# A hybrid block on one core: the first four units spread by TensorE, the last feed-forward product in four parts, three exponential buffers, new places

## The chip, the core and the metric

One core of a Trainium2 chip runs the whole program. Its engines are TensorE (PE, matmuls into PSUM), VectorE (DVE), ScalarE (ACT), GpSimd (POOL) and SyncE (SP, which here only issues DMAs). They run side by side and wait for each other by semaphores. PSUM has eight banks of 128 x 512 fp32. The metric is the time of one execution on the device in microseconds; the median of several runs counts.

## What is computed

The input x has 4 batches of 1024 rows and 128 channels. Three kinds of layer follow each other, each behind a layer norm and added to x:

```
x = x + attn(layernorm(x), Wq, Wk, Wv, Wo)          # 16 heads of 8; window of 32 and every 64th key, causal
x = x + ffn(layernorm(x), k0, k1, k2, s0, s1, s2)   # 256 -> 512 -> 512 -> 128, weights +1 or -1, relu * 2
x = x + mamba(layernorm(x), ...)                    # itself x + res_scale * out
x = x + ffn(layernorm(x), k0, k1, k2, s0, s1, s2)   # the same weights again

# mamba: 256 inner channels, 16 states, over 1024 steps
u, z = split(norm(x) @ W_in);  u2 = silu(conv(u) + conv_b)
dt_lo, B, C = split(u2 @ W_xp);  dt = softplus(dt_lo @ W_dt + b_dt)
h[t] = exp(dt[t] * A) * h[t-1] + (dt[t] * u2[t]) * B[t];  y[t] = sum over states of h[t] * C[t]
out = ((y + u2 * D) * silu(z)) @ W_out
```

## The kernel before

The work is cut by batches b and by halves of 512 rows (m = 2b + h, eight of them). Attention of a batch runs in 24 units u, with 128 x 512 scores each. A feed-forward pass f covers 512 rows (there are 17, the last two of half the size): transposed rows, first layer (fl1, four products over mo), second layer (fl2, four outputs mo with 8 fp16 matmuls each), last product (fl3, fp32) and the sum into X (fl3_v).

The scan of a half runs in 32 units, 256 in all. A unit holds 8 channels x 16 states on 128 partitions and 512 steps. For each unit: dt8_d reads the channels' step sizes from DRAM, spread over 16 partitions each, into DT (6 slots, NT); du8_d does the same for the inputs dt * u2 into D (12 slots, ND). decay_s (ACT, L1574) makes exp(dt * A) in one of the banks 0 and 1. The drive multiplies the inputs by B: drive_v on DVE (L1252), for 9 of 32 units drive_p on POOL (L1739). scan_v (DVE, L1264) runs the recurrence in place; out_p (POOL, L1752) multiplies two units by C; csum_t (PE, L951) sums over states into bank 2. Ahead of it stands, for each half and block eb of 128 channels: dt_t (PE, L936), dt_s, dt_v, dt_p, dr_v (the sizes, in sR), du_p (POOL, L1732, sR * u2, in sE), and dt_d and du_d, which write sR and sE to DRAM, from where dt8_d and du8_d read.

In an attention unit asc_t makes the scores (L764 the mask, L787 or L792 the products), asc_v (DVE, L1134, L1140) the maxima and for odd units the shift, asb_t (PE, L806) the shift of even units, asc_s (ACT, L1411) the exponentials into Sx, atr_t (PE, L815) the transposes, atr_s (ACT, L1418) their copy into PT, and apv_t (L832) the products with the values. Sx and PT have two buffers each. warm_t (L998) are idle products of two constants, whose result nobody reads.

The order of the instructions of each engine is written out: PLACES holds for each step a list of numbers, one for each time it occurs (a place), WARM the idle products as (place, bank, how many). timetable() sorts all by number, and each engine issues its own steps in that order. No engine goes past a step that waits. The products of PE take their banks in turn from a ring, from dt_t(0, 0) on the four banks 4 to 7; the turn waits until the bank's last content was read.

The last product of a pass waits for all four outputs of the second layer:

```
bank = bank_of["fl3", i] = turn((v_fx, i + 1))
eng.wait_ge(s_f2, 4 * i + 4)
for k in range(N // 128):
    for ki in range(4):
        t = eng.matmul(bank[:, 128 * k:128 * k + 128], h1[:, ki, 128 * k:128 * k + 128], w2[:, ki, :],
                       start=(ki == 0), stop=(ki == 3))
```

## Time and profile before

| | |
|---|---|
| median of 3 runs | 799.41 us (798.85 to 801.10) |
| the profiled execution | 800.71 us |
| its span, first to last instruction | 798.9 us |
| instructions | 22483 |
| busy: PE, DVE, ACT, POOL | 710.9, 689.1, 617.5, 601.3 us |
| mean granted clock of PE | 0.981 |
| moved by DMA | 154.95 MB, mean 194 GB/s |

A window of the trace gives the busy time of each engine in a stretch, the granted clock of PE as a share of 2.4 GHz, and what DMA moved. A row of the timeline is one instruction or a run of the same ones, with its start, its length and, in brackets, how long the engine was idle before it and which engine's work ended that. The chain is followed back from the last instruction. An fp32 matmul stands in the trace as two PE instructions. A line number is that of the kernel before; in the changed kernel the same code stands 15 to 46 lines further down.

### The profile page before, as it was taken

To read this page: it belongs to the slowest core of one execution; us is meant where nothing else is said; L and a number is where in the kernel's file an instruction comes from. 1 tells how busy PE (TensorE), PEld (TensorE's weight loads), DVE (VectorE), ACT (ScalarE), POOL (GpSimd) and SP (SyncE) were. 2 spreads that over 40 slices of the span, in tenths; PEclk is the share of its full clock that TensorE was granted. 3 is DMA by queue.
4 is the path that set the end of the run, shared out by engine and by line. 5 is a ranking of instruction groups with operands and counts; after the bars stand their busy time and mean duration, and the time that the engine had idled before them with its cause. 6 is when DMAs were issued, how large, how long until landed. Compare 5 with 4: busy or idle time off the path is not lost. (4 is left out here: it accounts for less than half of the span.)

```text
span 798.9 us, 22483 instructions
## 1 busy us (share of the span) xinstructions
PE 710.9 (89%) x8144; PEld 420.1 (53%) x8144; DVE 689.1 (86%) x1145; ACT 617.5 (77%) x1227; POOL 601.3 (75%) x591
## 2 busy tenths in 40 slices
PE   7998998998789999999999998998998989697788
PEld 5675655645565446547555364445454555262346
DVE  6887127999999989999899989999999898798983
ACT  4775789889769998999689989887778656754533
POOL 3032345879988989769897799799798999898671
PEclk9999999999999999999999999999999999798989
DMA  6000019997987769786968799978897989899860
GB/s 204 3 3 2 2 45 244 255 236 224 269 218 198 176 173 270 202 216 184 232 185 237 215 241 255 229 222 242 222 248 215 269 245 256 225 244 255 213 156 27
DMA packets 84176, 154.95 MB, mean 194 GB/s; under 512 B 9433, under 2 KB 10082, under 8 KB 84066
## 3 DMA queue, kind: packets, MB, share of 16 engines
q1 hardware_dynamic: 84066, 153.51, 71.7%
q8 instruction: 65, 1.06, 0.6%
q14 instruction: 45, 0.37, 0.2%
HBM read 142.47 MB, written 11.01 MB: 192 GB/s over the span
## 5 line engine op out<-in xcount | busy, mean ns | idle before, releaser
L1752 POOL TENSOR_TENSOR d<-d,cr 128x1024 f32<-128x1024 f32 x128 | 300.4, 2354 | 34.1 <-DVE d L1264 24.4
L1574 ACT ACTIVATE ps<-dt,An 128x512 f32<-128x512 f32 x256 | 173.7, 690 | 53.6 <-DVE d L1264 39.8
L1264 DVE TENSOR_TENSOR_SCAN d<-ps,hl,d 128x512 f32<-128x512 f32 x128 | 157.8, 1267 | 8.6 <-ACT ps L1574 7.1
L1264 DVE TENSOR_TENSOR_SCAN d<-ps,d 128x512 f32<-128x512 f32 x128 | 150.5, 1206 | 7.4 <-ACT ps L1574 4.4
L877 PE MATMUL ps<-h,w 128*128 128x512 f16 (+1 forms) x512 | 121.8, 392 | 11.2 <-DVE h L1208 9.6
L1252 DVE TENSOR_TENSOR d<-ps,d 128x512 f32<-128x512 f32 x184 | 118.4, 673 | 2.1 <-DMA d<-dud 1.9
L1739 POOL TENSOR_TENSOR d<-d,br 128x512 f32<-128x512 f32 x72 | 91.4, 1276 | 13.2 <-DMA d<-dud 13.1
L877 PEld LDWEIGHTS ps<-h,w 128*128 128x128 f16 x512 | 49.1, 101 | 85.8 <-DVE h L1208 21.7
L951 PE MATMUL ps<-d,cst 128*32 128x512 f32 x512 | 70.5, 625 | 11.4 <-POOL d L1752 8.3
L815 PE MATMUL ps<-cst,sx 128*128 128x128 f32 x384 | 55.4, 279 | 10.9 <-ACT sx L1411 5.5
L888 PEld LDWEIGHTS ps<-w,h 128*128 128x128 f32 x496 | 56.7, 192 | 7.8 <-ACT h L1477 6.1
L888 PE MATMUL ps<-w,h 128*128 128x128 f32 x496 | 58.9, 277 | 1.8 <-ACT h L1477 1.8
L916 PE MATMUL ps<-xnT,Wk 128*128 128x512 f32 x128 | 56.9, 594 | 1.7 <-ACT xnT L1509 0.9
L1418 ACT COPY pt<-ps 128x512 f32<-128x512 f32 x96 | 53.4, 590 | 5.8 <-PE ps L815 3.6
L815 PEld LDWEIGHTS ps<-cst,sx 128*128 128x128 f32 x384 | 41.8, 141 | 28.6 <-issue 9.4
L1477 ACT ACTIVATE h<-ps 128x512 f32<-128x512 f32 (+1 forms) x64 | 35.7, 580 | 23.1 <-PE ps L877 22.7
L998 PEld LDWEIGHTS ps<-cst 128*128 128x128 f32 x352 | 44.4, 199 | 15.8 <-issue 9.2
L1134 DVE TENSOR_REDUCE mn<-ps 128x8 f32<-128x512 f32 x64 | 41.4, 679 | 12.9 <-PE ps L792 12.7
L998 PE MATMUL ps<-cst 128*128 128x128 f32 x352 | 48.4, 288 | 4.5 <-DMA cst<-in_w 4.5
L832 PEld LDWEIGHTS ps<-v,pt 128*32 128x32 f32 x3072 | 34.1, 110 | 31.8 <-issue 29.2
L1397 ACT COPY v<-ps 32x256 f32<-32x256 f32 (+1 forms) x96 | 41.9, 436 | 11.2 <-PE ps L742 6.2
L832 PE MATMUL ps<-v,pt 128*32 128x18 f32 (+1 forms) x3072 | 39.8, 191 | 8.9 <-issue 3.2
(177 smaller groups left out, 1337.7 us busy)
## 6 DMA issues: line engine op xcount, KB each, us to landing
dt<-dtd SPq DMA_DIRECT2D x256, 256.0 KB, 5.3
d<-dud SPq DMA_DIRECT2D x256, 256.0 KB, 5.3
dtd<-sR SPq DMA_DIRECT2D x16, 256.0 KB, 3.6
dud<-sE SPq DMA_DIRECT2D x16, 256.0 KB
X<-in_x SPq DMA_DIRECT2D x8, 256.0 KB, 6.1
br<-bcd SPq DMA_DIRECT2D x8, 256.0 KB, 3.3
cr<-bcd SPq DMA_DIRECT2D x8, 256.0 KB, 3.7
out<-X SPq DMA_DIRECT2D x3, 512.0 KB, 5.6
```

Source lines behind the costliest of these rows:

```text
L815: t = eng.transpose(bank[:, 128 * k:128 * k + 128], sx[:, 128 * k:128 * k + 128], ident)
L832: t = eng.matmul(bo[32 * j:32 * j + 32, at, a, :], pt[:, i, 32 * j:32 * j + 32], V[:, 2 * kk + w, :, 4 * (2 * c + a) + j, :], start=True, ...
L877: t = eng.matmul(bank[:, 0:N], w1[:, ki, 128 * mo:128 * mo + 128], h0[:, s, ki, 0:N], start=(ki == s == 0), stop=(ki == 3 and s == 1))
L888: t = eng.matmul(bank[:, 128 * k:128 * k + 128], h1[:, ki, 128 * k:128 * k + 128], w2[:, ki, :], start=(ki == 0), stop=(ki == 3))
L916: t = eng.matmul(bank[:, :], Wk[:, k, 128 * eb:128 * eb + 128], xnT[:, 1 + k:513 + k], start=(k == 0), stop=(k == KC - 1))
L951: t = eng.matmul(bank[32 * q:32 * q + 32, :], csel[:, 24 - 8 * w:56 - 8 * w], D[:, (4 * k + q) % ND, :], start=(w == 0), stop=(w == 3))
L998: eng.matmul(banks[k][:, 0:128], ident, ident, start=True, stop=True)
L1252: eng.tensor_tensor(d, PB[:, :], d, ALU.mult).then_inc(v_dr, 1)
L1264: eng.tensor_tensor_scan(d, banks[u % NG][:, :], d, hl[:, r:r + 1] if m % 2 else 0.0, ALU.mult, ALU.add).then_inc(v_sc, 1)
L1574: eng.activation(banks[u % NG][:, :], DT[:, u % NT, :], ACT.Exp, scale=An[:, g:g + 1]).then_inc(s_da, 1)
L1739: eng.tensor_tensor(d, d, BR[m % 2][:, :], ALU.mult).then_inc(p_dr, 1)
L1752: eng.tensor_tensor(d, d, CR[m % 2][:, :].unsqueeze(1).to_broadcast((128, n, 512)), ALU.mult).then_inc(p_cm, n)
```

## The change

It has five parts.

1. For the units 0 to 3 (FIRST = 4) the step sizes and inputs no longer go through DRAM. A constant "spread" is added; bdt_t and bdu_t multiply 32 partitions of it with the same 32 of sR or sE, so that a bank holds what dt8_d or du8_d would have brought. decay_s reads the one bank, drive_v the other, all four drives are on DVE (those of units 0 and 1 were on POOL). dt8_d and du8_d run from unit 4 on.
2. fl3_t is cut in four parts, one for each output of the second layer, each with its own wait and its own place; the bank is taken by the first.
3. Sx and PT have three buffers (NS).
4. The idle products are set anew: 35 groups with 238 products, 33 groups with 176 before.
5. All places are new.

```
+FIRST = 4
+def driver(u):
+    return "v" if u < FIRST or u % NR not in DRIVEN_P else "p"
+def landed(u, n):
+    return u // n + 1 - (u % n < FIRST)
...
-    (CORE, 'decay_s dt8_d du8_d scan_v'),
+    (CORE, 'decay_s scan_v'),
+    (CORE[FIRST:], 'dt8_d du8_d'),
+    (CORE[:FIRST], 'bdt_t bdu_t'),
...
+    put("spread", (p[:, None] % 32 == p[None, :] % 8).astype(np.float32))
...
-        Sx = [sb(f"sx{i}", [128, 512]) for i in range(2)]
-        PT = [sb(f"pt{i}", [128, 4, 128]) for i in range(2)]
+        NS = 3
+        Sx = [sb(f"sx{i}", [128, 512]) for i in range(NS)]
+        PT = [sb(f"pt{i}", [128, 4, 128]) for i in range(NS)]
...
-            def fl3_t(f):
+            def fl3_t(f, mo):
...
-                bank = bank_of["fl3", i] = turn((v_fx, i + 1))
-                eng.wait_ge(s_f2, 4 * i + 4)
+                if mo == 0:
+                    bank_of["fl3", i] = turn((v_fx, i + 1))
+                eng.wait_ge(s_f2, 4 * i + mo + 1)
                 for k in range(N // 128):
...
+                    t = eng.matmul(bank_of["fl3", i][:, 128 * k:128 * k + 128], h1[:, mo, 128 * k:128 * k + 128], w2[:, mo, :],
+                                   start=(mo == k == 0), stop=(mo == 3), skip_group_check=True)
+                if mo == 3:
+                    t.then_inc(t_f3, 1)
...
+            def bdt_t(u):
+
+                bank = bank_of["bdt", u] = turn((s_da, u + 1))
+                eng.wait_ge(v_md, 2)
+                q = slice(32 * u, 32 * u + 32)
+                eng.matmul(bank[:, :], spread[q, :], sR[q, :], start=True, stop=True).then_inc(t_bdt, 1)
+
+            def bdu_t(u):
+
+                bank = bank_of["bdu", u] = turn((v_dr, u + 1))
+                eng.wait_ge(p_md, 3)
+                q = slice(32 * u, 32 * u + 32)
+                eng.matmul(bank[:, :], spread[q, :], sE[q, :], start=True, stop=True).then_inc(t_bdu, 1)
...
+                if u < FIRST:
+
+                    eng.wait_ge(v_set, V_END)
+                    eng.wait_ge(l_br, 32)
+                    eng.wait_ge(t_bdu, u + 1)
+                    eng.tensor_tensor(d, bank_of["bdu", u][:, :], BR[0][:, :], ALU.mult).then_inc(v_dr, 1)
+                    return
...
+                if u < FIRST:
+                    eng.wait_ge(t_bdt, u + 1)
+                    src = bank_of["bdt", u]
```

The waits of asc_v, asc_s and atr_s look back three units in place of two. The next dr_v waits until all four bdt_t are done, the next dt_s until all bdu_t are.

**First place: DVE around the first scans.** L1134, L1140 and L1150 are attention of batch 1, L1236 and L1245 the sizes, L1202 and L1208 feed-forward pass 1, L1252 drives, L1264 scans. Before:

```order
L1134 TENSOR_REDUCE zf<-ps 128x2x8
L1140 TENSOR_TENSOR sx<-ps,zf 128x512
L1236 TENSOR_SCALAR sT<-sE 128x512
L1264 SCALAR_TENSOR_TENSOR d<-ps,d 128x512 x2
L1202 TENSOR_TENSOR h<-ps,h 128x512
L1245 SCALAR_TENSOR_TENSOR sR<-ps,sL 128x512
L1252 TENSOR_TENSOR d<-ps,d 128x512 x2
L1208 SCALAR_TENSOR_TENSOR h<-ps,h 128x512 x3
L1264 SCALAR_TENSOR_TENSOR d<-ps,d 128x512 x2
```

In the changed kernel (L1287 the drives of the first four units, L1291 the other drives, L1303 scans, L1180, L1164 and L1170 the attention, L1266 sizes):

```order
L1287 TENSOR_TENSOR d<-ps,br 128x512
L1303 SCALAR_TENSOR_TENSOR d<-ps,d 128x512
L1287 TENSOR_TENSOR d<-ps,br 128x512 x3
L1303 SCALAR_TENSOR_TENSOR d<-ps,d 128x512 x3
L1180 STREAM_TRANSPOSE fc<-zf 128x256 x2
L1164 TENSOR_REDUCE zf<-ps 128x2x8 x2
L1170 TENSOR_TENSOR sx<-ps,zf 128x512
L1266 TENSOR_SCALAR sT<-sE 128x512
L1291 TENSOR_TENSOR d<-ps,d 128x512 x3
```

Four drives and four scans now stand ahead of the second round of reductions and of the sizes' second block; five more drives and all of pass 1's first layer stand between scan 3 and scan 4.

**Second place: PE in the same stretch.** L998 are idle products, L843 the attention's output, L815 and L832 transposes and value products, L764 and L787 scores, L806 the shift. Before:

```order
L843 MATMUL ps<-wgt,jt 128x128 x4
L806 MATMUL ps<-zf,cst 128x512
L998 MATMUL ps<-cst 128x128 x5
L815 MATMUL ps<-cst,sx 128x128 x8
L832 MATMUL ps<-v,pt 32x4x9 x32
L764 MATMUL ps<-masks,e 128x512 x2
L787 MATMUL ps<-KD,qm 64x2x32 x32
L737 MATMUL ps<-cst,lna 128x128 x2
L806 MATMUL ps<-zf,cst 128x512
L815 MATMUL ps<-cst,sx 128x128 x8
```

In the changed kernel (L959 is bdt_t, L966 bdu_t, L1028 the idle products):

```order
L1028 MATMUL ps<-cst 128x128 x7
L959 MATMUL ps<-sR,cst 128x512
L847 MATMUL ps<-v,pt 32x4x9 x32
L959 MATMUL ps<-sR,cst 128x512
L779 MATMUL ps<-masks,e 128x512 x2
L802 MATMUL ps<-KD,qm 64x2x32 x32
L966 MATMUL ps<-sE,cst 128x512
L821 MATMUL ps<-zf,cst 128x512
L959 MATMUL ps<-sR,cst 128x512
L966 MATMUL ps<-sE,cst 128x512 x3
L830 MATMUL ps<-cst,sx 128x128 x8
L959 MATMUL ps<-sR,cst 128x512
```

The eight new products stand in six places between those of the attention, four of them ahead of the transposes of units 2 and 3.

**Third place: PE in the last fifty microseconds**, from the first layer of pass (3, 2, 0) on. L866 is the first layer, L877 the second, L951 the sum over states, L981 the last half's output product, L998 idle. Before:

```order
L998 MATMUL ps<-cst 128x128 x3
L866 MATMUL ps<-h,w 128x512 x8
L951 MATMUL ps<-d,cst 32x512 x4
L877 MATMUL ps<-h,w 128x512 x8
L951 MATMUL ps<-d,cst 32x512 x4
L877 MATMUL ps<-h,w 128x512 x24
L981 MATMUL ps<-w,u 128x128 x8
```

In the changed kernel (L881, L892, L981 and L1011 are the same four, L1028 idle):

```order
L1028 MATMUL ps<-cst 128x128 x4
L881 MATMUL ps<-h,w 128x512 x6
L1028 MATMUL ps<-cst 128x128 x9
L881 MATMUL ps<-h,w 128x512 x2
L1028 MATMUL ps<-cst 128x128 x10
L892 MATMUL ps<-h,w 128x512 x8
L1028 MATMUL ps<-cst 128x128 x15
L981 MATMUL ps<-d,cst 32x512 x4
L1028 MATMUL ps<-cst 128x128 x8
L981 MATMUL ps<-d,cst 32x512 x4
L892 MATMUL ps<-h,w 128x512 x24
L981 MATMUL ps<-d,cst 32x512 x4
```

Four more groups of idle products stand between the layers and the sums over states. In the first pass the scores (L764, L792) that stood between the second layer and the last product now stand ahead of the second layer. On SP the first reads of inputs, eight in a row, stand ahead of the first five reads of sizes; before, the two kinds alternated by twos and threes.

## Rows read from the trace of the kernel before

**Rows 1.** Windows: length, busy of PE, PEld, DVE, ACT, POOL; clock, DMA, GB/s.

```profile
0.00:125.00 125.00, 110.90 (x1842) 75.36 (x1842) 73.77 (x214) 88.22 (x194) 40.71 (x81) 1.00 0.15 49
125.00:775.00 650.00, 580.56 (x6157) 328.40 (x6143) 606.88 (x906) 521.48 (x1013) 557.47 (x502) 0.98 0.86 228
775.00:799.00 24.00, 19.48 (x164) 16.32 (x160) 8.44 (x25) 7.82 (x22) 3.12 (x8) 0.99 0.07 23
...
75.00:100.00 25.00, 24.67 (x252) 14.83 (x251) 6.04 (x16) 15.97 (x37) 7.01 (x18) 1.00 0.01 3
```

**Rows 2.** Timeline around the first scan: start, length, engine, line, operation, idle before.

```profile
117.61 1.28 POOL L1732 TENSOR_TENSOR sE<-sR,u 128x512 f32<-128x512 f32 x1 [0.80 <-DVE sR L1245]
...
123.14 1.16 SPq L686 DMA_DIRECT2D d<-dud  x2
126.35 2.50 POOL L1739 TENSOR_TENSOR d<-d,br 128x512 f32<-128x512 f32 x2 [3.03 <-DMA d<-dud]
129.94 2.33 DVE L1264 TENSOR_TENSOR_SCAN d<-ps,d 128x512 f32<-128x512 f32 x2
...
141.88 5.67 DVE L1264 TENSOR_TENSOR_SCAN d<-ps,d 128x512 f32<-128x512 f32 x5
```

**Rows 3.** A product dt_t in the timeline; eight convolution products on the chain.

```profile
111.18 1.09 PE L936 MATMUL ps<-lnm,Wdt 9*128 9x512 f32 x2 [0.42 <-ACT lnm L1538]
...
589.22 7.14 PE ps L916 x16
```

**Rows 4.** Scans and drives on DVE: ns of one, least, median, most.

```profile
L1264 DVE TENSOR_TENSOR_SCAN d<-ps,d x128: 1181/1209/1224, 129.9 to 704.6; 128x512 f32<-128x512 f32 x128
...
L1252 DVE TENSOR_TENSOR d<-ps,d x184: 626/677/692, 133.5 to 770.3; 128x512 f32<-128x512 f32 x184
```

**Rows 5.** Windows before the first scan, columns as in rows 1.

```profile
110.00:120.00 10.00, 8.20 (x161) 5.88 (x164) 3.59 (x10) 7.92 (x18) 5.24 (x5) 1.00 0.29 95
120.00:130.00 10.00, 8.47 (x178) 5.45 (x169) 5.81 (x16) 9.35 (x23) 4.97 (x8) 1.00 0.80 221
```

**Rows 6.** Idle before L888 and before L1418: until whom, us, times.

```profile
  ACT h L1477: 8.0, 8
...
  PE ps L832: 1.9, 3
```

**Rows 7.** Timeline of the first pass' second layer, last product, and what follows.

```profile
74.39 7.42 PE L877 MATMUL ps<-h,w 128*128 128x512 f16 x32
...
82.97 3.84 PE L888 MATMUL ps<-w,h 128*128 128x128 f32 x32
...
88.93 0.20 POOL L1710 TENSOR_SCALAR mr<-mmv 128x4 f32<-128x4 f32 x1 [17.20 <-DVE mmv L1018]
```

**Rows 8.** Timeline at the end: the last products of the last two passes.

```profile
792.41 1.95 PE L888 MATMUL ps<-w,h 128*128 128x128 f32 x16
792.62 0.39 ACT L1477 ACTIVATE qm<-ps 128x256 f32<-128x256 f32 x1 [0.49 <-PE ps L877]
```

**Rows 9.** Windows in which the granted clock is low, columns as in rows 1.

```profile
695.00:700.00 5.00, 4.24 (x11) 1.09 (x11) 5.00 (x8) 2.96 (x6) 4.49 (x4) 0.55 0.97 257
...
735.00:740.00 5.00, 5.00 (x20) 2.06 (x19) 1.97 (x3) 2.36 (x4) 2.19 (x1) 0.79 0.71 177
...
765.00:770.00 5.00, 5.00 (x18) 1.92 (x19) 5.00 (x5) 2.95 (x6) 5.00 (x4) 0.72 1.06 278
```

**Rows 10.** Pieces of the chain that ended last: start, us, engine, line, instructions.

```profile
569.29 7.02 PE ps L877 x32
...
706.61 2.90 PE ps L998 x26
...
731.56 8.93 PE ps L877 x28
```

**Rows 11.** Waits that nothing in the profile explains: us, times, longest us.

```profile
PEld ps L832 <- issue: 29.2, 54, 1.6
...
PEld ps L916 <- issue: 28.6, 116, 0.8
```

More of the change, by code:

```diff
@@ L23 @@
 CONST, NCONST = {}, 0
-for _name, _n in (("ident", 128), ("qmask", 4), ("csel", 56), ("one8", 1), ("rmask", 2)):
+for _name, _n in (("ident", 128), ("qmask", 4), ("csel", 56), ("one8", 1), ("rmask", 2), ("spread", 128)):
     CONST[_name] = (NCONST, _n)
@@ L98 @@
 DRIVEN_P = [0, 1, 5, 9, 13, 17, 21, 25, 29]
-def driver(r):
-    return "p" if r in DRIVEN_P else "v"
+FIRST = 4
+def driver(u):
+    return "v" if u < FIRST or u % NR not in DRIVEN_P else "p"
 def driven(u, by):
-    return u // NR * sum(driver(r) == by for r in range(NR)) + sum(driver(r) == by for r in range(u % NR))
+    return sum(driver(x) == by for x in range(u))
+def landed(u, n):
+    return u // n + 1 - (u % n < FIRST)
 def rows_of(f):
@@ L165 @@
     (BATCH_HALVES[2:], 'aln_v'),
-    ([(u,) for u in range(NCORE) if driver(u % NR) == "v"], 'drive_v'),
+    ([(u,) for u in range(NCORE) if driver(u) == "v"], 'drive_v'),
     (BLOCKS[:-1], 'gate_p yev_v'),
@@ L170 @@
     (BATCHES, 'aap_p akp_p'),
-    ([(u,) for u in range(NCORE) if driver(u % NR) == "p"], 'drive_p'),
+    ([(u,) for u in range(NCORE) if driver(u) == "p"], 'drive_p'),
     (PAIRS, 'out_p'),
@@ new lines @@
+    "dt_d": [113425, 141515, 180593, 210290, 271266, 290303, 353024, 387904, 439657, 458170, 505869, 544136, 592186, 622015, 671561,
+        692352],
+    "dt_p": [108041, 128368, 176237, 193326, 267819, 282512, 349577, 381280, 436210, 454211, 499855, 521343, 588739, 613711, 663358,
+        680096],
+    "dt_s": [106237, 126564, 174273, 190652, 266015, 280058, 347200, 379476, 434406, 450904, 497816, 518533, 586730, 609305, 661175,
+        674950],
+    "dt_t": [105083, 125410, 172709, 189498, 264861, 278678, 346046, 378322, 433252, 449750, 496662, 517379, 585576, 608151, 660021,
+        673423],
@@ new lines @@
+    "jrec_v": [54404, 101414, 206452, 252936, 360000, 376022, 529030, 597673],
+    "jsub_p": [50292, 88764, 184030, 247009, 337633, 369290, 511222, 587438],
+    "jsum_p": [53249, 99796, 204659, 251335, 356344, 374376, 520264, 596182],
+    "jtr_v": [58941, 107911, 211559, 258000, 366902, 386442, 536731, 606332],
+    "jx_v": [60945, 111370, 216511, 262806, 371764, 391528, 538653, 608389],
+    "lg_v": [751325, 751667],
+    "lm_t": [751809, 752256],
+    "lm_v": [752453, 753633],
+    "lmo_t": [748155, 749045],
@@ new lines @@
+    "lpre_p": [720809],
+    "mln_p": [83973, 148557, 244002, 294859, 410981, 459343, 562604, 637007],
+    "mln_s": [88821, 154887, 248961, 300602, 415846, 472845, 568082, 641378],
+    "mln_t": [88527, 154172, 248527, 300077, 415506, 472140, 568261, 641532],
+    "mln_v": [82682, 146581, 242353, 292727, 409690, 458052, 561313, 635716],
+    "mno_s": [86748, 151332, 246777, 297924, 413756, 468771, 565379, 639782],
+    "mout_t": [218347, 291850, 382829, 459439, 563687, 620002, 695437],
+    "mout_v": [221838, 293933, 385799, 461522, 568662, 624329, 698659],
@@ L475, in const @@
             return cst[0:rows, at:at + n]
-        ident, qmask, csel, one8, rmask = (const(n) for n in ("ident", "qmask", "csel", "one8", "rmask"))
+        ident, qmask, csel, one8, rmask, spread = (const(n) for n in ("ident", "qmask", "csel", "one8", "rmask", "spread"))
         masks = sb("masks", [128, 288], BF16)
@@ L879, in fl2_t @@
                 t.then_inc(t_f2, 1)
-            def fl3_t(f):
+            def fl3_t(f, mo):
                 i = FFN_AT[f]
                 _, _, _, h1, N = room(f)
-                bank = bank_of["fl3", i] = turn((v_fx, i + 1))
-                eng.wait_ge(s_f2, 4 * i + 4)
+                if mo == 0:
+                    bank_of["fl3", i] = turn((v_fx, i + 1))
+                eng.wait_ge(s_f2, 4 * i + mo + 1)
                 for k in range(N // 128):
-                    for ki in range(4):
-                        t = eng.matmul(bank[:, 128 * k:128 * k + 128], h1[:, ki, 128 * k:128 * k + 128], w2[:, ki, :],
-                                       start=(ki == 0), stop=(ki == 3))
-                t.then_inc(t_f3, 1)
+                    t = eng.matmul(bank_of["fl3", i][:, 128 * k:128 * k + 128], h1[:, mo, 128 * k:128 * k + 128], w2[:, mo, :],
+                                   start=(mo == k == 0), stop=(mo == 3), skip_group_check=True)
+                if mo == 3:
+                    t.then_inc(t_f3, 1)
             def mln_t(m):
@@ L1119, in asc_v @@
                 nw = 8 if kind else 4
-                bank, sx = bank_of["sc", b, u], Sx[U % 2]
+                bank, sx = bank_of["sc", b, u], Sx[U % NS]
                 sv = bank[:, :].rearrange("p (a w k) -> p a w k", a=2, w=nw)
```

232 lines of the change are left out of this document (107 added, 125 removed), and 319 rows, old and new, of tables (PLACES, WARM).

## The prediction

> **What bounds the kernel now.** I first read the busy times of the engines in three long stretches [rows 1]. Up to 125 us VectorE (DVE) is busy 73.8 us and TensorE (PE) 110.9. From 125 to 775 us DVE is busy 606.9 of 650 us, PE 580.6, GpSimd (POOL) 557.5 and ScalarE (ACT) 521.5. The last 24 us hold short products and small steps. In the window from 75 to 100 us PE is busy 24.67 of 25 and DVE 6.04 [rows 1]. So PE and the attention chains set the time up to the first scan, and after it the list of DVE does, with 256 scans and a drive for most of them. The queues run in the order written by the table of places: a hole of one engine is filled only if the table puts work there. Of DVE's 110 us of idle time, 51 lie before 125 us (125 - 73.8), 43 between 125 and 775 (650 - 606.9), 15.6 behind.
>
> **Part 1, units 0 to 3 on another way.** Their sizes and inputs now go from sR and sE to DRAM and come back spread over 128 partitions. In the trace sE is ready at 117.61 + 1.28 = 118.9 us, the first read of inputs is issued at 123.14, POOL's first drive starts at 126.35 after 3.03 us of waiting, the first scan at 129.94 [rows 2]. In the changed kernel one product with "spread" puts each tile into a bank: 118.9 plus one product. The nearest row for one with few rows of contraction is that of dt_t, 9 rows high: 1.09 us with its latency [rows 3]. So drive 0 can start near 120.0 and scan 0 near 120.8, nine us earlier. That is not nine us of gain, since the work only moves into DVE's holes. Moved are four scans and the drives 2 and 3: 4 x 1.209 + 2 x 0.677 = 6.2 us [rows 4]; drives 0 and 1 come anew from POOL, 1.35 us. Together 7.5 us have to go between 120 and 130 us, where DVE is idle for 10 - 5.8 = 4.2 us [rows 5]. 3.3 us of other DVE work (the score reductions of batch 1, and pass 1) is pushed behind 130. Net 6.2 - 3.3 = **2.9 us**. Bounds: 6.2 if holes before 120 take the rest, 0 if PE can't deliver (a rival, below).
>
> PE gets 8 products more. Back to back such a product takes 0.89 us (16 instructions, 8 products, in 7.14) [rows 3], 7.1 us in all, in a stretch from 110 to 130 where it is idle for 20 - 16.7 = 3.3 us [rows 5]. So its own queue comes 3.8 us late there. That is the same 3 to 4 us of attention and pass 1 that DVE pushes back anyway; the two overlap, and I count them once. POOL loses two drives, which is free, because it waited for them [rows 2]. On SyncE (SP) the eight first reads of inputs now stand ahead of the sizes of unit 4. First read to first drive took 3.2 us [rows 2]; if each read behind it adds 1.2 us (256 KB at the 221 GB/s of the window from 120 to 130 [rows 5]), unit 4's sizes land at about 122 + 3.2 + 9.6 = 135 us. Scan 4 started at 141.88 [rows 2]: covered by some 6 us.
>
> **Part 2, the last product in four parts.** The matmuls stay in number. What goes is PE's wait for the fourth activation: ahead of L888 PE was idle for 8.0 us in 8 cases until h of L1477 was there [rows 6]. In the first pass attention scores fill that wait: the last L877 runs out at 74.39 + 7.42 = 81.8, L888 starts at 82.97, and POOL stands idle 17.20 us until the sums behind it are there [rows 7]. In the changed kernel these scores stand ahead of the second layer and the first part can follow at once: **1.2 us** earlier. Bounds 0 and 1.2, since PE is full there [rows 1] and the order decides who profits. In later passes DVE is mostly the late one: of the 8.0 us I take **0.5**, bounds 0 and 6. At the very end nothing: PE runs L888 from 792.41 on without a hole, the fourth activation (792.62) is covered by the other pass's products [rows 8]. Against it: the bank is held from the first part on, one of four in the ring.
>
> **Part 3, three buffers for exponentials.** The wait this can take away is that of the copy L1418 for L832 two units back, 1.9 us in 3 cases [rows 6]. I take **0.5**, bounds 0 and 1.9, and, if freer orders bring more, 3.
>
> **Part 4, idle products.** 176 become 238, nearly all new ones in the last sixth: from place 641,000 on 56 before and 117 now. The granted clock shows what they meet: 0.55 from 695 to 700 us, 0.79 from 735 to 740, 0.72 from 765 to 770 [rows 9]. On the chain a second-layer instruction takes 219 ns at full clock (32 in 7.02) and 319 in the stretch from 731.56 (28 in 8.93), 2.8 us more [rows 10]. In the two other stretches DVE is busy 5.00 of 5, so a faster PE gives little there; from 735 to 740 it is busy 1.97 [rows 9], so the 2.8 can be had. The bound is three such stretches, 8.4. The price: an idle product is two instructions, 0.223 us (26 in 2.90, on the chain) [rows 10]; with 6 more on the path 1.3. Net **1.5 us**, bounds 8.4 gained and, with all 61 on the path, 13.6 lost.
>
> **The other places.** Many rows of the four queues change places by a few. No row prices this; I take 0, and 3 us to both sides for the range.
>
> **The sum.** 2.9 + 1.2 + 0.5 + 0.5 + 1.5 = 6.6 us. The profiled execution took 800.7 us, so 794.1; it lies 1.3 above the median of 799.4, so the forecast is **792.8 us**.
>
> **The rivals.** *The scans keep their whole lead* (A): 6.2 for part 1, and 2.8 for part 4 with no price. 6.2 + 1.2 + 0.5 + 0.5 + 2.8 = 11.2 gives 788.2. For it: DVE is busy only 3.59 of the 10 us before 120 [rows 5]. Against it: the inputs don't exist before 118.9.
>
> *PE can't deliver the spread tiles* (B). They are products of 32 rows between products of 128. Where the shape of the tile changes PE stands with nothing to wait for: 29.2 us in 54 cases before L832, 0.54 a time, against 28.6 in 116, 0.25, before L916, whose shape stays [rows 11]. The eight stand in six places of the queue: 3 us more on top of the 3.8. Attention of batch 1 and pass 1 then come 7 us late, which eats part 1's 6.2. With part 4 at 0 the sum is 6.2 - 7 + 1.2 + 0.5 + 0.5 = 1.4, the time 798.0: no change. Against it: dt_t, 9 rows high between 128-row products, took 1.09 us as a whole [rows 3]. The Trainium skill has a rule for this (TensorEngine Tiling (Array Packing), Key Properties): changing the tiling mode drains TensorE, while tiles of one mode work in parallel. By that rule the eight cost six drains, and the three that stand in a row are nearly free, which takes 2 us off. The gap before L832 agrees with a drain; no row here shows 32-row tiles side by side.
>
> *The idle products lie on the path* (C), the case that ends slower. Near the end four groups of 9, 10, 15 and 8 stand directly ahead of first- and second-layer products and sums. If what comes behind is ready by then, PE works them off first. All 61 are 13.6 us; against gains of 2.9 + 1.2 + 0.5 + 0.5 + 2.8 = 7.9 that is 5.7 slower, 805.1. It turns slower by 0.3% once more than 46 of the 61 (10.3 us) are on the path. For it: 13 are on the chain now [rows 10]. Against it: PE is idle 69 us from 125 to 775 [rows 1], so most can lie in holes.
>
> **How the numbers follow.** The forecast 0.53, A 0.20, B 0.15, C 0.12. A measurement of this kernel can tell about 0.3% from no change, 2.4 us. Forecast and A are faster, B within, C mostly slower; a little of the forecast's case and of C falls within 0.3%: faster 0.73, same 0.16, slower 0.11. The forecast's own range is 789.5 to 796.5. For 8 in 10 it goes down to 787.5, which takes in A, and up to 799.5, which takes in B.
>
> **What would show it.** Part 1: first scan at 119 to 123 us, the fifth not before 133; DVE's hole between 115 and 125 filled; its idle time from there to the last scan near the 43 us of now, and the last scan some 6 us earlier. Part 2: L903 (L888 before) in the first pass right behind the second layer. Part 4: clock above 0.9 in the windows from 685 to 770, and 219 ns for a second-layer instruction. It is wrong if PE has no hole from 110 to 130 and DVE waits for reductions there (B), if idle products have more than 4 us on the chain (C), or if the scans' lead at unit 32 is gone at unit 200: then the new places lost elsewhere what the first units gained.

## The result, and the profile after

The changed kernel takes **810.67 us** (median of 4 runs, 807.97 to 813.30), the kernel before 799.82 beside it: 1.0134 of it, 95% interval 1.0086 to 1.0182. It is 11 us slower, where 6.6 us less were forecast. Its runs lie in two groups, 808 us at a mean granted clock of 0.976 to 0.979 and 813 us at 0.964 to 0.966. The profiled execution is one of the first (808.20 us, span 806.4, which is 7.5 more than before).

The three long stretches, as [rows 1] (length, busy of PE, PEld, DVE, ACT, POOL; clock, DMA, GB/s):

```profile
0.00:125.00 125.00, 113.25 (x1818) 76.38 (x1818) 76.39 (x226) 88.61 (x196) 39.26 (x82) 1.00 0.16 50
125.00:775.00 650.00, 590.89 (x6263) 345.16 (x6264) 598.63 (x891) 513.39 (x1003) 550.06 (x497) 0.97 0.84 223
775.00:799.00 24.00, 20.49 (x165) 15.56 (x163) 14.47 (x31) 10.29 (x25) 8.86 (x11) 1.00 0.18 60
```

From 125 to 775 us DVE is busy 598.6 us, 8.3 less than before: new holes, not new work. They are few. Worked out from both traces, the start of each scan less its place in the table (in us) is the lag of the plan:

```
                     scan 4 (start)   last scan (start)   jumps of the lag by over 3 us
kernel before         5.2  (141.9)    16.7  (772.2)       none
changed kernel       11.6  (147.1)    31.7  (779.9)       7.1 at scan 4, 3.7 at scan 98 (399), 3.5 at scan 222 (given back), 4.7 at scan 252 (775)
```

The new table puts the last scan 7 us earlier; execution loses 15 us more against it than before, in three places.

**The first units.** The timeline of the changed kernel around scans 0 to 4, by start, length, engine, line, and idle time before:

```profile
122.95 1.32 PE L966 MATMUL ps<-sE,cst 32*128 32x512 f32 x6
126.57 1.12 PE L959 MATMUL ps<-sR,cst 32*128 32x512 f32 x2
129.28 1.16 PE L802 MATMUL ps<-KD,qm 64*64 64x64 f32 x64
135.17 1.86 PE L952 MATMUL ps<-lnm,Wdt 9*128 9x512 f32 x2 [4.73 <-issue]
...
126.01 3.69 DVE L1303 TENSOR_TENSOR_SCAN d<-ps,d 128x512 f32<-128x512 f32 x3
138.51 0.43 DVE L1266 TENSOR_SCALAR sT<-sE 128x512 f32<-128x512 f32 x1 [5.95 <-ACT sE L1590]
147.05 2.33 DVE L1303 TENSOR_TENSOR_SCAN d<-ps,d 128x512 f32<-128x512 f32 x2
...
137.15 0.60 ACT L1588 ACTIVATE sE<-ps 128x512 f32<-128x512 f32 x1 [6.18 <-PE ps L952]
```

The spread products do what was wanted: 1.12 us for one alone, three in a row in 1.32, scans 0 to 3 done by 129.7 us, where before [rows 2] two were done by 132.3. Then PE stands for 4.73 us ahead of dt_t(0, 1) (L952), with "issue" as the reason: the profile shows no semaphore that it waits for. ACT and DVE wait 6 us for it, and scan 4 starts 5.2 us later than before. Behind the hole PE also runs slower; L952 takes 1.86 us, not 1.09 as in [rows 3]. The windows there:

```profile
125.00:130.00 5.00, 4.46 (x128) 3.14 (x132) 4.86 (x7) 4.27 (x11) 2.44 (x2) 1.00 1.06 256
130.00:135.00 5.00, 0.44 (x32) 0.48 (x23) 2.35 (x5) 0.95 (x3) 2.62 (x3) 0.83 1.05 258
135.00:140.00 5.00, 4.61 (x8) 1.53 (x7) 1.49 (x3) 2.04 (x4) 0.98 (x1) 0.50 0.09 22
```

After 0.44 us of PE in 5 the granted clock falls to 0.50 of 2.4 GHz, its level of 1.2. DMA was full until the hole ended. The DMA view of 119 to 133 us (reads with KB each and us from issue to landing), and of 132.3 to 132.6 (packets, MB, share):

```profile
d<-dud SPq DMA_DIRECT2D x8, 256.0 KB, 5.1
dt<-dtd SPq DMA_DIRECT2D x5, 256.0 KB, 8.7
```

```profile
q1 hardware_dynamic: 46, 0.08, 115.1%
q8 instruction: 1, 0.02, 26.2%
```

Thirteen reads are issued from 120.7 to 128.9 us. By their landings 8 of them are under way at most (at 128 us) and 5 at 132.3, and among their packets is one of kind "instruction", which starts at 132.35 us, 2.8 us before PE goes on. The page counts 66 of this kind on queue q8. Two later holes of this kind are in the middle of work that waits for nothing, the second inside one group of 64 matmul records (an fp32 product is two):

```profile
217.04 1.12 PE L821 MATMUL ps<-mn,cst 128*128 128x512 f32 x2 [1.93 <-issue]
...
386.63 0.44 PE L847 MATMUL ps<-v,pt 128*32 128x18 f32 x31
389.27 0.76 PE L847 MATMUL ps<-v,pt 128*32 128x18 f32 x33 [2.19 <-issue]
```

An earlier one of 1.86 us stands where no data moves. The DMA view of 51 to 57 us has a single packet, one of instructions, and then PE's row:

```profile
DMA packets 1, 0.02 MB, mean 3 GB/s; under 512 B 0, under 2 KB 0, under 8 KB 0
...
56.28 0.61 PE L847 MATMUL ps<-v,pt 128*32 128x18 f32 x45 [1.86 <-issue]
```

**The end.** PE, SP and DVE from 761 us on, and two windows:

```profile
761.57 1.89 PE L892 MATMUL ps<-h,w 128*128 128x512 f16 x4 [3.38 <-DVE h L1238]
763.25 4.26 PE L1028 MATMUL ps<-cst 128*128 128x128 f32 x30
767.44 1.06 PE L981 MATMUL ps<-d,cst 128*32 128x512 f32 x8
768.43 2.05 PE L1028 MATMUL ps<-cst 128*128 128x128 f32 x16
...
768.57 2.61 SPq L701 DMA_DIRECT2D d<-dud  x3
...
772.77 0.69 DVE L1291 TENSOR_TENSOR d<-ps,d 128x512 f32<-128x512 f32 x1 [3.58 <-DMA d<-dud]
775.18 2.45 DVE L1303 TENSOR_TENSOR_SCAN d<-ps,hl,d 128x512 f32<-128x512 f32 x2
```

```profile
760.00:765.00 5.00, 3.43 (x13) 2.47 (x14) 5.00 (x7) 2.41 (x6) 2.76 (x2) 0.66 0.87 209
765.00:770.00 5.00, 5.00 (x45) 4.04 (x44) 4.19 (x5) 2.48 (x5) 4.36 (x3) 1.00 0.04 9
```

Fifteen idle products (L1028) stand ahead of a sum over states (L981) and take 4.26 us. The sum releases D's buffers; only then, at 768.57, SP issues the last reads of inputs, and DVE waits for them. DMA's share from 765 to 770 us is 0.04; the same window of before has 1.06 [rows 9]. That is the mechanism of rival C, near the end alone.

### The profile page after: what moved, and what is told of

Read it like the earlier page. It is cut to its first block and busy times, and to the rows that moved or that the text cites. A ratio compares the mean times of both kernels' runs of the same rounds, so it can differ in the third digit from the quotient of the medians.

```text
span 806.4 us, 22760 instructions
## 1 busy us (share of the span) xinstructions
PE 729.3 (90%) x8284; PEld 441.3 (55%) x8284; DVE 690.0 (86%) x1147; ACT 613.8 (76%) x1227; POOL 598.2 (74%) x589
## 5 line engine op out<-in xcount | busy, mean ns | idle before, releaser
L1620 ACT ACTIVATE ps<-dt,An 128x512 f32<-128x512 f32 x252 | 170.7, 691 | 59.9 <-DVE d L1303 43.1
L1303 DVE TENSOR_TENSOR_SCAN d<-ps,hl,d 128x512 f32<-128x512 f32 x128 | 157.8, 1266 | 4.4 <-ACT ps L1620 2.6
L1303 DVE TENSOR_TENSOR_SCAN d<-ps,d 128x512 f32<-128x512 f32 x128 | 150.5, 1206 | 6.5 <-ACT ps L1620 4.9
L892 PE MATMUL ps<-h,w 128*128 128x512 f16 (+1 forms) x512 | 118.0, 382 | 7.3 <-DVE h L1238 6.7
L1291 DVE TENSOR_TENSOR d<-ps,d 128x512 f32<-128x512 f32 x182 | 117.3, 671 | 5.9 <-DMA d<-dud 5.9
L1785 POOL TENSOR_TENSOR d<-d,br 128x512 f32<-128x512 f32 x70 | 88.8, 1275 | 19.9 <-DMA d<-dud 16.1
L892 PEld LDWEIGHTS ps<-h,w 128*128 128x128 f16 x512 | 47.6, 99 | 80.9 <-DVE h L1238 17.5
L981 PE MATMUL ps<-d,cst 128*32 128x512 f32 x512 | 69.6, 619 | 7.7 <-POOL d L1798 7.2
L1028 PEld LDWEIGHTS ps<-cst 128*128 128x128 f32 x476 | 59.4, 200 | 18.2 <-issue 10.2
L1028 PE MATMUL ps<-cst 128*128 128x128 f32 x476 | 63.4, 287 | 5.3 <-DMA cst<-in_w 5.3
L903 PEld LDWEIGHTS ps<-w,h 128*128 128x128 f32 x496 | 58.5, 193 | 8.4 <-issue 5.3
L903 PE MATMUL ps<-w,h 128*128 128x128 f32 x496 | 60.4, 278 | 0.9 <-ACT h L1516 0.7
L1164 DVE TENSOR_REDUCE mn<-ps 128x8 f32<-128x512 f32 x64 | 41.3, 678 | 5.1 <-PE ps L807 4.9
L1450 ACT ACTIVATE sx<-ps 128x512 f32<-128x512 f32 x48 | 28.4, 591 | 21.3 <-PE ps L821 21.0
L1238 DVE SCALAR_TENSOR_TENSOR h<-ps,h 128x512 f16<-128x512 f32 (+1 forms) x64 | 39.4, 662 | 6.0 <-ACT h L1510 5.8
```

The costliest lines, as they stand in the source:

```text
L892: t = eng.matmul(bank[:, 0:N], w1[:, ki, 128 * mo:128 * mo + 128], h0[:, s, ki, 0:N], start=(ki == s == 0), stop=(ki == 3 and s == 1))
L903: t = eng.matmul(bank_of["fl3", i][:, 128 * k:128 * k + 128], h1[:, mo, 128 * k:128 * k + 128], w2[:, mo, :], start=(mo == k == 0), stop=( ...
L981: t = eng.matmul(bank[32 * q:32 * q + 32, :], csel[:, 24 - 8 * w:56 - 8 * w], D[:, (4 * k + q) % ND, :], start=(w == 0), stop=(w == 3))
L1028: eng.matmul(banks[k][:, 0:128], ident, ident, start=True, stop=True)
L1291: eng.tensor_tensor(d, PB[:, :], d, ALU.mult).then_inc(v_dr, 1)
L1303: eng.tensor_tensor_scan(d, banks[u % NG][:, :], d, hl[:, r:r + 1] if m % 2 else 0.0, ALU.mult, ALU.add).then_inc(v_sc, 1)
```

## Where PE stands: one position of its code

The trace has one 16 KB instruction packet on q8 for every 256 records of PE (17032 records, 66 packets; matmuls, weight loads and semaphore waits counted). So I numbered PE's records in order and added up its idle time by position modulo 256. In the changed kernel position 193 holds 11.6 us, the next one 3.4, apart from the wait for the first inputs at the very start. Every hole above stands there: the one at 56 us ahead of record 7 x 256 + 193, at 135 us 15 x 256 + 193, at 217 us 22 x 256 + 193, at 389 us 39 x 256 + 193. In none of the 20 traces (the two kernels and the 18 experiments below) does PE get past record 256 n + 193 sooner than 2.2 us behind the start of packet n; after a hole of over 0.9 us it goes on 2.3 to 3.3 us behind. In the kernel before the same position holds 2.5 us. All idle time of PE that the profile puts down to "issue" is 4.8 us before and 13.6 after.

The traces also hint at when a packet is asked for. No packet n starts more than 42 records ahead of record 256 (n - 1) + 193, and in the median it starts 1.0 to 2.2 us behind it (19 traces; 0.5 in the one whose mean clock is 0.554); so the next packet is asked for, as far as this tells, about when PE gets past the boundary before. Ahead of the hole near 135 us the packet started 4.7 us behind that record, while PE worked the 256 records off in 2.9 us.

**Theory, late code**: PE's instructions arrive by the same DMA engines as the data, 256 at a time. If PE works through a dense stretch (many short products), it runs out of instructions, the more so when reads of data hold the packet up. Where it runs out is set by the count of all instructions ahead, so any edit moves it. **Rivals**: the eight spread products hold PE up (B); idle products are the whole loss (C).

## Experiments: the two causes

All times are set beside runs of the kernel before on the same chip; the chip differs between groups of experiments, so the ratios compare better than the times; "of before" is the ratio with its 95% interval. P193 is the idle time at that position in the run's trace.

**Reads drawn apart.** Four of the eight first du8_d behind the sizes, and in dt8_d:

```
+                if u == 6:
+                    eng.wait_ge(v_sc, 4)
```

> The changed kernel with the first reads of SyncE drawn apart: four of the eight first reads of inputs (units 8 to 11) stand behind the reads of sizes, and the third read of sizes waits for the fourth scan, so that some six reads of 256 KB and not thirteen are outstanding between 121 and 131 us. Late code (PE's packets of instructions queue behind the data): PE's hole of 4.7 us ahead of dt_t(0, 1) (L952) shrinks below 1.5 us, scan 4 starts near 142 and not 147 us, and the median falls by 5 to 7 us, to 804 to 806. PE can't deliver the spread tiles (B): hole and time stay within 1 us. Idle products on the path: nothing changes here, since it acts near 765 us.

Measured: 808.99 us, 1.0106 of before (1.0060 to 1.0152). The hole ahead of dt_t(0, 1) is gone (P193 7.2 us), scan 4 starts at 145.2. The time fell by 1.7 us and not by 5 to 7, with intervals that overlap. In the profiled run PE was at half clock from 117 to 134 us, and a spread product took 2.07 us, so that scan 3 came 3 us later. At that clock PE needed 4.0 us for the 256 records ahead of the boundary and not 2.9, so this run alone doesn't show that the reads made the hole. The run with both edits below does: full clock up to 132 us, the same reads, and 1.71 us of hole.

**Idle group out.**

```
-    (735961, 2, 15), (739046, 4, 8), (757905, 5, 4),
+    (739046, 4, 8), (757905, 5, 4),
```

> The changed kernel without the group of 15 idle products ahead of csum_t(60), nothing else. Idle products on the path: the 4.3 us of these products at a clock of 0.66 vanish, the last reads of inputs are issued some 4 us earlier and the median falls by 4 to 5 us, to 806 or 807. If they buy clock for what stands behind them, the sums and layers behind run slower by as much and the time stays within 1 us. Late code: the hole near 135 us stays as it is; since 30 instructions fewer come at 765 us, no boundary of a packet before that moves.

Measured: 809.62 us, 1.0120 (1.0061 to 1.0179). That can't be told from the changed kernel; 4 to 5 us less were expected. In its trace the plan's lag jumps by 1.5 us at scan 252, not 4.7: the end is repaired, and more was lost ahead of it (the runs spread from 806 to 815 us). A second expectation missed: nothing differs ahead of 765 us, and yet the hole near 135 us did not stay as it was:

```profile
134.13 1.86 PE L952 MATMUL ps<-lnm,Wdt 9*128 9x512 f32 x2 [1.33 <-issue]
```

PE was at half clock there from 124.0 to 144.5 us and needed 4.9 us for the 256 records. Scan 4 started at 148.1, later than with the hole of 4.73. So one trace says little on the length of a hole, and here a slow PE cost scan 4 as much as a hole.

**Boundary moved by taking 13 idle products out.**

```
-    (8848, 2, 8), (10191, 0, 3), (102142, 5, 5), (108670, 7, 6), (111520, 2, 7), (197534, 4, 1), ...
+    (8848, 2, 8), (10191, 0, 3), (102142, 5, 5), (197534, 4, 1), ...
```

> The changed kernel without the 13 idle products at the places 108,670 and 111,520, which fed nothing: 52 PE instructions (each product stands for a weight load and a matmul, in fp32 two of each) fewer ahead of dt_t(0, 1), so that every later packet of 256 instructions begins 52 instructions further on in the program. Late code: the hole of 4.7 us no longer stands ahead of dt_t(0, 1) (L952) but some 50 instructions behind it or is much smaller, the holes in the value products at 389 us and ahead of the shift at 217 us move as well, and the median changes by 2 to 6 us, likely down. If PE waits for a semaphore or for the drain of a changed tile shape at L952, the hole stays ahead of L952 with its 4 to 5 us. Idle products on the path: within 1 us.

Measured: 815.43 us (four runs within 1.4), 1.0186 (1.0152 to 1.0219). The hole ahead of L952 is gone; holes now stand at 165.3 us (1.77) and 397.0 (2.31), again at 193 (P193 7.9 us). The direction of the time was missed, for another reason. The windows from 110 us, and a spread product:

```profile
110.00:115.00 5.00, 2.85 (x18) 1.82 (x16) 1.05 (x2) 4.94 (x12) 2.85 (x3) 1.00 0.41 118
115.00:120.00 5.00, 3.92 (x68) 1.64 (x68) 3.34 (x12) 2.85 (x8) 3.79 (x9) 0.75 0.29 108
120.00:125.00 5.00, 5.00 (x70) 2.90 (x70) 2.29 (x4) 2.37 (x5) 1.93 (x5) 0.50 0.74 204
...
118.03 2.07 PE L959 MATMUL ps<-sR,cst 32*128 32x512 f32 x2
```

Without these idle products PE is busy 2.85 us of 5 and the clock falls to half just where the first units run; the time is 4.8 us longer (this median less that of the changed kernel), with 3.7 us less at P193. That the missing products made the clock fall isn't shown. The run with the reads apart has all of them, PE is busy 4.65 of 5 us from 110 to 115, and the clock fell at the same place:

```profile
115.00:120.00 5.00, 5.00 (x134) 3.29 (x134) 2.26 (x10) 2.47 (x6) 4.34 (x12) 0.69 0.30 108
120.00:125.00 5.00, 5.00 (x10) 1.79 (x10) 3.10 (x4) 2.82 (x8) 0.05 (x1) 0.50 0.87 221
```

**Both edits together.**

> The reads drawn apart and the group of 15 idle products taken out, together. Both causes hold and are independent: 5 to 7 and 4 to 5 us less than the changed kernel, near 799 us, which is the time of the kernel before. Only one of the two holds: 803 to 807.

Measured: 801.55 us (10 runs), 1.0019 (0.9997 to 1.0040): 9 us less than the changed kernel, between the 799 expected of two causes and the 803 to 807 of one. They don't add up as independent causes would: alone the edits gave 1.7 and 1.1 us. No run shows why. The half clock may be part of it: the profiled runs of the two single edits had 17 and 20 us of it near 130 us, this one 3.4. P193 is 11.0 us, hardly less than the 11.6 of the changed kernel, so the sum of the holes doesn't set the time by itself. Scan 4 starts at 141.9, as before. What is left of the first hole:

```profile
130.94 1.01 PE L954 MATMUL ps<-lnm,Wdt 9*128 9x512 f32 x2 [1.71 <-issue]
```

## Experiments: the same order, another boundary

These add tiny products of constants and change nothing else. Behind the first idle group of the kernel before, 36 of them (144 instructions), or 16 (64):

```
+                if (k, products) == (2, 8):
+                    for _ in range(36):
+                        eng.matmul(banks[k][0:32, 0:8], ident[0:32, 0:32], ident[0:32, 0:8], start=True, stop=True)
```

> The kernel before with 36 tiny products of constants (32x32 by 8 columns, four PE instructions each) behind its first group of idle products, while PE waits for input anyway: 144 PE instructions more ahead of everything, no order, wait or buffer changed. In the traces so far PE's stalls without a semaphore stand at instruction 256 n + 193 of its stream, whatever the kernel, and each ends 2.5 to 2.8 us behind the start of a 16 KB packet of instructions. In the kernel before PE's own work takes over 4 us from instruction 256 n - 64 to 256 n + 193 in all but one or two places; moved by 144 there are several dense stretches (transposes, value products, scores) at that spot. Late code: the stalls at 256 n + 193 sum to 6 us or more (2.5 us in the kernel before) and the time rises by 3 to 8 us. If the order or waits make the stalls: at most 1.5 us more, the price of the 144 tiny instructions.

> The kernel before with 16 tiny products (64 PE instructions, 1.1 us) at the same spot. Late code: the stalls at 256 n + 193 rise from 2.5 to 6 us or more, and the time by 4 to 12 us, since of the shifts worked out from the trace all from 40 to 230 put dense stretches ahead of the boundary. If 144 was an odd case: 801 to 803.

Measured: with 144 instructions **825.26 us**, 1.0367 (1.0312 to 1.0421), P193 17.8 us; with 64, 811.27 us, 1.0160 (1.0138 to 1.0182), P193 7.5 us. The tiny products themselves cost 2.9 us with 144 (the scores of unit 0 start at 19.09, not 16.21) and nothing with 64 (16.18). With 144 the loss is far above the 3 to 8 us expected. The hole near 135 us stands inside one group of 64 score products (L787). First the run with 144, then with 64:

```profile
131.27 0.56 PE L787 MATMUL ps<-KD,qm 64*64 64x64 f32 x18
137.84 1.55 PE L787 MATMUL ps<-KD,qm 64*64 64x64 f32 x46 [6.01 <-issue]
```

```profile
128.87 1.14 PE L787 MATMUL ps<-KD,qm 64*64 64x64 f32 x58
133.17 0.34 PE L787 MATMUL ps<-KD,qm 64*64 64x64 f32 x6 [3.16 <-issue]
```

Behind the 18th matmul record of the group the one time, behind the 58th the other: 40 matmuls, each with its weight load, make 80 records, which is 144 - 64. No wait, shape or bank can do that. This settles where PE stands.

> The changed kernel with 36 tiny products (144 PE instructions) behind its first idle group, just as in the kernel before that went from 800 to 825 us. If the old order only stands at a lucky boundary and the new one is otherwise as good: 810 to 825 us, no slower than 825. If the new order is worse by itself by the 10 us of the main result: 835 us or so.

Measured: the changed kernel with 144 takes 814.93 us, 1.0202 (1.0175 to 1.0230), P193 9.6. At this boundary the changed kernel is 10 us faster than the kernel before (13 by the two ratios), with 8.2 us less at P193; at its own it is 11 us slower. The kernel before stands at a good boundary: both its shifts are slower by 11 and 25 us, those of the changed kernel by 4 and 7.

> The changed kernel with 12 such tiny products behind the idle group at place 111,520: 48 PE instructions more from 112 us on, nothing else. Late code: PE's stalls ahead of L952 (4.7 us), at 217 us (1.9) and at 389 us (2.2) vanish or shrink below 1 us, since the spots 256 n + 193 then come behind longer stretches; one near 397 us may come in their place. The median falls by 4 to 8 us. Otherwise: no change beyond 1 us. Idle products on the path near 765 us: untouched, 4 to 5 us stay.

> The changed kernel with all three edits: first reads drawn apart, the group of 15 idle products out, 48 PE instructions more from 112 us on. Late code: of the stalls at 256 n + 193 of the version without the shift (1.6 us at 131, 2.5 at 214, 1.6 at 289, 1.9 at 389, 0.7 at 397, at least 7 us) most go, of which DVE passes on 3 to 5 us, for 797 to 799 us: faster than the kernel before. If alignment of the code doesn't matter: 801 to 802 us as without the shift.

Measured: 817.80 us, 1.0241 (1.0201 to 1.0280), and 812.92 us, 1.0150 (1.0110 to 1.0190). Both expectations missed. The first hole went as expected (scan 4 at 144.6), but the boundary fell into another dense group (P193 14.3 and 13.7 us). In the first of the two:

```profile
392.46 0.70 PE L847 MATMUL ps<-v,pt 128*32 128x18 f32 x61
397.83 0.29 PE L847 MATMUL ps<-v,pt 128*32 128x18 f32 x3 [4.66 <-issue]
```

I had counted how long PE needs for the 256 records ahead of a boundary, but not how late the packet is at that time; so a good shift couldn't be read from density alone.

## Experiments: the queue ahead of the code

A cap: each dt8_d and du8_d first waits until the fourth read ahead of it has landed.

```
+            def few(slot, u, n):
+                if len(issued) >= 4:
+                    eng.wait_ge(*issued[-4])
+                issued.append((slot, 16 * landed(u, n)))
```

> The kernel before with one thing added: each read of sizes or inputs waits until the fourth read ahead of it has landed, so that never more than four reads of 256 KB are outstanding. Late code: PE's stalls at instruction 256 n + 193 are only 2.5 us here, so the time changes little, within 2 us of the kernel before. If the cap starves the units of data: slower by 2 us or more, with DVE and ACT waiting for DMA.

> The changed kernel with the same cap of four outstanding reads, nothing else. Late code behind a queue of reads: the stall of 4.7 us ahead of L952 shrinks below 1.5, those at 217 and 389 us below 1 us each; the median falls by 4 to 8 us, to 803 to 807. If the code is late for a reason other than the reads: no change of the stalls.

> The kernel before with 144 tiny instructions ahead (825 us, 17.8 us of stalls at 256 n + 193, of which one of 6.0 and six of 1 to 2.5) and the cap. Late code behind a queue of reads: the stalls fall to 8 us or less and the time to 812 or below; what is left, some 3 us, is the price of the tiny instructions and the fetch itself where the code is dense. If only the place of the boundary counts and not the reads: within 2 us of 825.

Measured: the kernel before with the cap 1.0022 (1.0008 to 1.0037); the changed kernel with it 804.93 us, 1.0091 (1.0059 to 1.0122); the one with 144 instructions 823.04 us, 1.0316 (1.0291 to 1.0341). The hole near 135 us in the changed kernel, and in the one with 144:

```profile
133.70 1.01 PE L961 MATMUL ps<-lnm,Wdt 9*128 9x512 f32 x2 [1.64 <-issue]
```

```profile
139.24 0.92 PE L796 MATMUL ps<-KD,qm 64*64 64x64 f32 x46 [1.92 <-issue]
```

4.73 became 1.64 and 6.01 became 1.92, and the hole at 389 us is gone (P193 7.2 of 11.6 us). The place of a hole is set by the boundary. On its length, the start of the packet says more than the hole: in the changed kernel it came 4.7 us behind record 256 (n - 1) + 193, with both edits 1.9, with the cap 1.8, each at full clock. So there the reads held it up. With 144 instructions it came 10.2 us behind, with the cap still 8.0; the hole is shorter mostly because PE, at half clock, needed 8.8 us for the records and not 6.9. The Trainium skill (DMA: Bandwidth & Descriptors, Queues, rings and completion order) says that each DMA engine goes round-robin between its queues, a packet at a time; by that rule code would never wait for a whole queue of reads. In the changed kernel the packet started some 3 us sooner behind fewer reads, so here it did wait for some of them; when it was asked for no row shows. With 144 the time fell by 2 us only, not 13, which is what was expected if only the place of the boundary counts: P193 is still 12.7 us, in eight holes of 0.8 to 2.8 us, and the clock is 0.51 from 130 to 135 us. What holds the packets up there isn't shown, and the hole of 1.86 us at 56 us shows that a short one needs no reads.

Without the group of 15 as well, and with the cap only at the four dense places (units below 20, 34 to 50, 58 to 72, 94 to 112), and then without the group of 8 too:

> The changed kernel with the cap and without the group of 15 idle products. Both causes: 9 to 13 us less than the changed kernel, 798 to 802; with the stalls at 214 to 397 us gone too, which drawing the first reads apart left in place, it can pass the kernel before, at 796 to 799.

> The changed kernel without the group of 15 idle products, at most six reads outstanding in place of four. If the cap of four starves the units (it cost the kernel before 0.2%): 1 to 2 us faster than with four, 0.997 to 1.001 of the kernel before. If six reads are long enough a queue to make the code late again: the stalls at 256 n + 193 grow from 6.4 to 8 us or more and the time rises by 1 to 3 us.

> The changed kernel without the group of 15, the cap of four only for the reads of the units below 20, 34 to 50, 58 to 72 and 94 to 112, which are issued around PE's four long stalls (135, 214, 290 and 389 us). Late code: the stalls stay near 6.4 us, the price of the cap elsewhere goes, 0.995 to 1.000 of the kernel before. If the change has no gain of its own: 1.001 to 1.005, as with the cap everywhere.

> The same without the next group of 8 idle products too (16 instructions, 2.05 us, between two sums over states at 768 us in the changed kernel). Idle products on the path: another 1 to 2 us less. If they keep the clock for the second layer behind them: no change or 1 us more, and a clock below 0.8 in the windows from 765 to 780.

```
                             us        of before                 P193
cap 4                        804.93    1.0091 (1.0059-1.0122)    7.2
cap 4, without 15            800.32    1.0024 (0.9994-1.0054)    6.4
cap 6, without 15            804.88    1.0080 (1.0056-1.0105)    -
cap 4 at dense places        800.65    1.0025 (1.0000-1.0049)    6.3
the same, without 15 and 8   799.44    1.0014 (0.9995-1.0034)    6.1
```

Taking the 15 idle products out is worth 4.6 us here (804.93 to 800.32; 4 to 5 were expected), the 8 another 1.2, less than its interval. Six reads in place of four cost 4.5 us by the ratios, which fits late code, but isn't shown: the only trace of this version is of an execution of 1176.77 us at a mean granted clock of 0.554, left out of its median. Position 193 holds 1.0 us in it, so a PE at about half speed hardly runs out of instructions. How PE passes the spot at the end, with the cap and the 15 idle products, then without:

```profile
758.80 1.89 PE L901 MATMUL ps<-h,w 128*128 128x512 f16 x4 [3.79 <-DVE h L1247]
760.49 5.52 PE L1037 MATMUL ps<-cst 128*128 128x128 f32 x30
765.93 1.06 PE L990 MATMUL ps<-d,cst 128*32 128x512 f32 x8
```

```profile
758.88 1.86 PE L901 MATMUL ps<-h,w 128*128 128x512 f16 x4 [2.94 <-DVE h L1247]
760.68 1.88 PE L990 MATMUL ps<-d,cst 128*32 128x512 f32 x8
```

No version beats the kernel before. The best of the changed ones is level with it, with 6 us of holes left against 2.5. Of the cap at dense places it was expected that the ratio lies between 1.001 and 1.005 if the change has no gain of its own, and below 1 if it has; 1.0025 came.

## Experiments: parts 2 and 3 alone

In the kernel before, the four parts of the last product in a row at its old place:

```
-                eng.wait_ge(s_f2, 4 * i + 4)
-                for k in range(N // 128):
-                    for ki in range(4):
+                for mo in range(4):
+                    eng.wait_ge(s_f2, 4 * i + mo + 1)
+                    for k in range(N // 128):
```

and, in a second kernel, three buffers Sx and PT besides.

> The kernel before with the last product cut in four parts that stand in a row at its old place, each with its own wait for one output of the second layer: part 2 of the change alone. As the prediction sized it, 0.5 to 1.7 us faster. If DVE's list is the bound at all 17 passes: within 0.5 us.

> The kernel before with the last product in four parts at its old place and three buffers for exponentials: parts 2 and 3 of the change alone. As sized, 1.2 + 0.5 (first pass and later ones) + 0.5 us less, 0.997 to 0.998 of the kernel before; with part 2 alone it was 0.9989. If part 3 brings nothing: 0.998 to 1.000.

Measured: 798.66 us, 0.9989 (0.9972 to 1.0006), and 799.25 us, 1.0011 (0.9989 to 1.0032). Part 2 may bring the 1 us of the forecast, which can't be told from none; part 3 brings nothing measurable.

## Why the prediction was wrong, point by point

**Part 1, 2.9 us.** The mechanism came as written: first scan at 122.98 (119 to 123 forecast), four scans out of the way, DVE busy 9.45 of 10 us from 120 to 130. Rival B fell: the scans kept their lead through unit 3, and PE stood at none of the eight products. Between neighbours of 128 rows they start 1.06 us apart (121.14 L821, 122.20 L959), where products of one shape take 0.89 [rows 3], so that a change of shape costs 0.2 us at most, not 0.54. The Trainium skill (TensorEngine Tiling (Array Packing), Key Properties) has each change of mode drain PE; the trace leaves room for 0.2 us of it at this place. That tiles of one mode work in parallel, the 1.32 us for three agree with.

**The step that failed** is the one on SP: "the eight first reads of inputs now stand ahead of the sizes of unit 4 ... covered by some 6 us". I asked of the burst only when its own data would land. That part came true: by the trace the sizes landed from 132.4 us on, where 135 was forecast. What shares the DMA engines with it, PE's code, was priced at nothing, and so was the clock behind a hole. In the profiled run this term is the 7.1 us at scan 4: 4.73 of hole, the rest PE at half clock behind it and the way through ACT and POOL. The run without the group of 15 lost 7.8 us there with 1.33 of hole and half clock from 124.0 us on; with both edits it is 3.2. The sign that the prediction named for its failure, a lead of the scans that is lost later, showed at once: scan 4 was already 5.2 us late.

**The other places, 0 with 3 to either side.** This term was mis-sized, not just unknown: with no step reordered, 64 or 144 instructions more move this kernel by 11 and 25 us. Rows 11 don't help here, and I read them wrongly for rival B. They are rows of the weight loads: during the 29.2 us ahead of L832 PE's matmuls were busy for 21.6, during the 28.6 ahead of L916 for 27.9, so that PE as a whole stood far less than 0.54 us at a change of shape. Only 1.6 of the 29.2 us lie at position 193.

**Part 2, 1.7 us.** Mechanism right. The idle time ahead of L903 until the fourth activation fell to 2.3 us from 8.0 [rows 6], and in the first pass L903 starts 1.0 us earlier than in [rows 7], POOL's next step 1.1 earlier:

```profile
  ACT h L1516: 2.3, 2
...
81.97 3.73 PE L903 MATMUL ps<-w,h 128*128 128x128 f32 x32
...
87.82 0.20 POOL L1756 TENSOR_SCALAR mr<-mmv 128x4 f32<-128x4 f32 x1 [16.80 <-DVE mmv L1048]
```

**Part 3, 0.5 us.** The wait it was to remove, 1.9 us in 3 cases [rows 6], is 3.4 in 3. It is worth nothing here.

**Part 4, 1.5 us.** The clock from 735 to 740 us rose to 1.00 from 0.79 [rows 9] as forecast; from 760 to 765 it is 0.66, and from 695 to 700 0.65, where above 0.9 was forecast. The price was sized by "6 more on the path", 1.3 us; it was 15, at low clock 4.3 us, then 4.6 between the two capped versions (1.1 from the changed kernel itself). Rival C had the mechanism and the place, with the wrong extent: 15 of the 61 matter, perhaps 23. What it would show (more than 4 us of idle products) is what came, though ahead of a sum, not on the chain at the end.

**The sum.** That the new order gains 6.6 us anywhere isn't shown. The table puts the last scan 7 us earlier, but that is the plan. At the shift of 144 the changed kernel is 10 us faster, but 8.2 of them are holes that it has less of there. With the cap and without the group of 15 it is level with the capped kernel before, with 5 us more of holes, which leaves room for a gain and doesn't prove it. From the forecast of 6.6 us less to the 10.9 us more there are 17.5. The two edits together gave back 9.1, so burst and group of 15 are about half of it; for the rest no run names a cause. How much of the holes reaches the end isn't settled either: with the two edits P193 was still 11.0.

## What to carry to other kernels

A few tiny instructions at the start, with no step reordered, moved the time of this kernel by 1.6 and 3.7% (0.4 of the latter is their own time), more than the change was to bring, through the places where PE's code runs out; before an edit is judged, move its boundary by some tiny instructions and measure again. Look for idle time of the matmuls (not of the weight loads) put down to "issue" inside a group of equal products, number the engine's records, and see whether the holes share a position. Compare the clock of two traces before the length of a hole. Keep bursts of reads away from dense stretches of PE; and put idle products where PE would wait, not ahead of a step that something waits for.

## What the runs showed of the hardware

- There is one 16 KB instruction packet for 256 records of PE, on the DMA engines that move the data. PE never passed record 256 n + 193 sooner than 2.2 us behind the start of packet n (20 traces), and stood up to 6.01 us there; 1.86 us even with no other packet in 6 us.
- A hole costs twice: behind one of 4.73 us the granted clock was 0.50 for the next 5 us, and dt_t took 1.86 us instead of 1.09.
- With the same instructions up to 765 us PE was at full clock until 133.3 us in one execution and at half clock from 124.0 in another. Thirteen idle products near 110 us did not keep it up: with them in place it was at half clock from 117 to 134 us in a third. Fifteen idle products ahead of a sum took 4.26 us, and 5.52 in the version with the cap, where the time is 4.6 less without them.
- 32-row products between 128-row ones took 1.12 us at full clock and 2.07 at half; a change of shape cost 0.2 us at most where it was read.
